# The order of turning and multiplying in the patch stage of a vision tower

## The reference, in short

```python
x = features.reshape(B, c, h, P1, w, P2)
x = jnp.transpose(x, (0, 2, 4, 3, 5, 1)).reshape(B, h * w, P1 * P2 * c)
x = _layernorm(x, ln1_g, ln1_b)
x = jnp.einsum('bnd,de->bne', x, W) + b     # 768 -> 192
x = _layernorm(x, ln2_g, ln2_b)
```

## Time and profile before

| | |
|---|---|
| time, median of 3 runs | 3089.83 us (3086.55 to 3103.68) |
| time of the profiled execution | 3087.19 us |
| its span, first to last instruction | 3085.5 us |
| mean granted TensorE clock | 0.961 |
| busy: TensorE, VectorE, ScalarE, GpSimd | 89%, 75%, 61%, 55% of the span |
| patch stage | to about 368 us |

### The profile page before, as it was taken

One profiled execution on the slowest core, in us unless ns is written; L12 is line 12 of the kernel. 1 busy time (PEld: TensorE's weight loads), 2 busy tenths in 40 slices (PEclk: granted clock), 3 DMA queues, 4 the chain that ended last, 5 costly groups with the idle time before them and its releaser, 6 DMA issues. The chain is left out here.

```text
span 3085.5 us, 95504 instructions
## 1 busy us (share of the span) xinstructions
PE 2732.0 (89%) x31491; PEld 2124.6 (69%) x31491; DVE 2311.9 (75%) x5326; ACT 1878.1 (61%) x3798; POOL 1682.0 (55%) x1957
## 2 busy tenths in 40 slices
PE   5798788999899998989998967999986999999998
PEld 5688645555555555555555546899975888888887
DVE  5689678788878887877788735877765777777776
ACT  5577556667666666666666636777753444444443
POOL 3467635555455666667666432567674444444444
PEclk9899989999999999999999968999987999999999
DMA  6555256676766667676767635444433444444443
GB/s 159 161 157 166 58 121 155 145 164 149 157 142 152 165 163 167 161 173 160 175 159 174 143 76 136 147 147 147 143 126 91 68 67 65 68 67 65 69 66 47
DMA packets 515433, 395.07 MB, mean 128 GB/s; under 512 B 223136, under 2 KB 488386, under 8 KB 515138
## 3 DMA queue, kind: packets, MB, share of 16 engines
q1 hardware_dynamic: 431426, 310.47, 41.3%
q0 software_dynamic: 38496, 46.38, 8.5%
q10 hardware_dynamic: 45216, 34.34, 4.6%
HBM read 232.59 MB, written 155.42 MB: 126 GB/s over the span
## 5 line engine op out<-in xcount | busy, mean ns | idle before, releaser
L814 DVE TENSOR_REDUCE a_mx<-a_mxp 98x4 f32<-98x784 f32 x768 | 747.0, 973 | 268.6 <-PE a_mxp L1000 265.9
L603 ACT ACTIVATE a_pt<-a_st 98x784 f32<-98x784 f32 x768 | 634.6, 826 | 352.8 <-PE a_st L986 351.9
L1817 POOL DMA_INDIRECT out_dram<-f_yo,f_idg x202 | 330.9, 1638 | 415.6 <-DVE f_yo L2158 378.9
L500 POOL TENSOR_TENSOR a_cf<-a_ctxs,a_rec 128x1176 f32<-128x1176 f32 x64 | 171.6, 2681 | 448.1 <-DMA a_rec<-a_recip 448.1
L1895 ACT ACTIVATE f_hf<-f_bank,f_b1c 128x256 f32<-128x256 f32 x606 | 254.3, 473 | 236.0 <-PE f_bank L1128 236.0
L1015 PE MATMUL a_pv<-a_pt,a_vp 98*32 98x196 f32 x6144 | 358.7, 352 | 5.0 <-issue 4.1
L986 PE MATMUL a_st<-a_qst,a_kst 49*128 49x196 f16 x3072 | 266.7, 253 | 78.6 <-DMA a_qst<-a_mrow 53.5
L2320 PE MATMUL f_bank<-f_w2h,f_hh 128*128 x1212 | 298.9, 247 | 19.0 <-DVE f_hl L2142 18.7
L2321 PE MATMUL f_bank<-f_w2h,f_hl 128*128 x1212 | 298.2, 246 | 0.0
L2322 PE MATMUL f_bank<-f_w2l,f_hh 128*128 x1212 | 298.2, 246 | 0.0
L1000 PE MATMUL a_mxp<-a_kst,a_qst 48*128 48x196 f16 x3072 | 263.6, 250 | 28.8 <-DVE a_mx L814 21.5
(11 more groups left out here) (314 smaller groups left out, 8269.9 us busy)
## 6 DMA issues: line engine op xcount, KB each, us to landing
a_rec<-a_recip SPq DMA_DIRECT2D x256, 147.0 KB, 4.9
t_rows<-in_x_dram SPq DMA_DIRECT2D x84, 392.0 KB, 5.7
a_qst<-a_qk SPq DMA_DIRECT2D x256, 110.2 KB, 3.2
a_kst<-a_qk SPq DMA_DIRECT2D x256, 110.2 KB, 4.0
f_xg<-f_listed SPq DMA_DIRECT2D x101, 264.0 KB, 2.8
a_qk<-a_qkh SPq DMA_DIRECT2D x128, 196.0 KB, 3.1
a_qk<-a_qkl SPq DMA_DIRECT2D x128, 98.0 KB, 3.4
a_qk<-a_qkh SPq DMA_DIRECT2D x128, 98.0 KB, 2.5
```

The costliest lines, as they stand in the source:

```text
L603: act.activation(pt[k % PT][:].rearrange("p j a t -> p j (a t)"), st_ps[0:half_t, :, 0:unit_t], ACT.Exp, scale=sm_scale).then_inc(exp_s, 1)
L814: dve.tensor_reduce(mx[:, a, :, 2 * p:2 * p + 2].rearrange("p q j -> p j q"), mx_ps[0:half_t, :, 0:unit_t].rearrange("p j (q t) -> p j q t ...
L1817: pool.indirect_dma_start(out, bass.IndirectOffsetOnAxis(ap=idg[i % 3][:, t:t + 1], axis=0), yo[i % 3][:, t, :], None, compute_op=ALU.add) ...
```

## The change

Within a step TensorE first turned both patches of unit s + 1 and then multiplied both patches of unit s. Now it turns patch 0, multiplies patch 0, turns patch 1, multiplies patch 1. All instructions, waits and signals stay; `yp_s` is still given once, behind the products of patch 1.

```diff
             def step(s, kinds):
-                if "B" in kinds:
-                    u = s + 1
-                    for t in range(2):
+                for t in range(2):
+                    if "B" in kinds:
+                        u = s + 1
                         wait(pe, xn_s, 2 * u + t + 1)
                         wait(pe, xl_s, 2 * (u - 1) + t + 1)
                         for k in range(KT):
                             a, kk = divmod(k, KT // 2)
                             ins = pe.transpose(turned[t][:, a, kk * R:(kk + 1) * R], xn[t][:, k * 128:(k + 1) * 128], ident[0:R, 0:R])
                         ins.then_inc(tr_s, 1)
-                if "C" in kinds:
-                    u, b = s, s % 2
-                    for t in range(2):
+                    if "C" in kinds:
+                        u, b = s, s % 2
                         wait(pe, xl_s, 2 * u + t + 1)
                         if t == 0:
                             wait(pe, yn_s, 2 * (u - 1))
                         ins = products(pe, yp[b][0:R, t * dim:(t + 1) * dim],
                                        [(x[b][t][:, k, :], m[:, k, :]) for k in range(KT) for x, m in ((xh, wh), (xh, wl), (xl, wh))]
                                        + [(first_two[:], brow_parts[:])])
-                    ins.then_inc(yp_s, 1)
+                        if t == 1:
+                            ins.then_inc(yp_s, 1)
```

## The result

| | before | after |
|---|---|---|
| median of 20 runs each | 3090.66 us (3072.61 to 3111.17) | 3109.22 us (3091.80 to 3122.66) |
| ratio after / before | | 1.0047, 95% interval 1.0026 to 1.0067 |
| profiled execution | 3087.19 us | 3092.7 us |
| its span | 3085.5 us | 3091.0 us |
| start of the first `yn` | 46.99 | 46.15 |

The change costs 0.47% by the ratio of the runs (14.5 us of 3090.66; the interval is 8 to 21 us); the two medians lie 18.6 us apart, inside that interval. The patch stage ends 12.8 us later. The single profiled execution hides it in part: its rest, which the change does not touch, happened to be 7.3 us shorter.

The account below looks back on a forecast made before the run. A closed GpSimd-ScalarE loop (4.94 us a clean step) was taken as the bound. Terms 0.4 + 1.5 + 2.0 + 12 + 0.1 = +16.0 us on the profiled 3087.2 gave 3103, range 3090 to 3120.

Parts of the forecast that it names:

- The new loop: ScalarE to TensorE and back, with patch 0's products ahead of T1, sets the step at 5.60 us.
- The signs: Middle stretch: expected waits of `xh`, `yn` and GpSimd, clean steps of 5.5 to 5.7 us, 39 steps about 230 us.
- The work beside: Middle stretch: weight preparation and next-stage first units on all engines, not covered by the longer loop, add 12 us.
- Filling: Start of the patch stage: the moved block delays the first steps, +0.4 us, between 0 and 1.57.
- Three steps before the weights: Steps from 46.99 until SyncE reaches the weights at 62.32: 15.33 us becomes 16.8, +1.5.
- Late rows: Third group's image rows, queued behind weight loads on SyncE, come about 2 us later; later steps before the stall are hidden.
- Restart: After the stall for image rows: a block of slow-clock products stands before T1, +2.0 us.
- Tail: Last steps of the patch stage: two steps lose what the shorter path to the last product returns, +0.1 us.
- The bound before: Before the change, GpSimd and ScalarE's `yn` wait for each other in a closed loop, 4.94 us a clean step.
- second rival: Middle stretch: work beside is not absorbed, 25.7 us on top and 3.9 for the ends, about 3117 us; chance 0.18.
- The clock: TensorE: no slow-clock cost taken for 1.2 us waits; a rival had fallback costing +29 us, 3132, chance 0.06.
- case 1: Likeliest outcome: the ScalarE-TensorE loop sets the step, 3096 to 3112 us, centre 3103; chance 0.60.

Follow-up runs that it names:

- e3: Changed kernel with 10 of patch 0's 19 products between the two turns, the other 9 behind the second turn; 3083.91 us (median of 12), ratio 0.9975.
- e4: Changed kernel with all 19 products of patch 0 and 10 of patch 1 between the two turns; 3148.53 us (one time).
- e8: Changed kernel with `yn` ahead of the second `xh` on ScalarE and the products' statistics ahead of the second `xl` on VectorE; 3102.55 us (one time).
- e7: Changed kernel with GpSimd computing scale and shift ahead of its work on `yn`; 3100.71 us (one time).
- after_again: Changed kernel without any edit, profiled a second time on another, slower chip; its 56th `yn` starts at 377.89 us.
- e2: Kernel before the change with `yn` placed between the first and the second `xh` on ScalarE; 3105.15 us (one time).
- e5: Kernel before the change with GpSimd computing scale and shift ahead of its work on `yn`; 3083.74 us (one time).

## Why the prediction was right

Direction, mechanism and size held: 3103 predicted, 3109.2 measured, +16 against +14.5 us (8 to 21; 18.6 between the medians). Of the 6 us between the times 3.5 are the starting point: the forecast counts from the one profiled execution (3087.2), and the median of 20 runs is 3090.66. That +16 lies so near is in part luck: the patch stage, to which all of its terms belong, ends 12.8 us later in the first pair of profiles and 9.6 in the second. By its steps:

- **The new loop.** Right, with 5.48 us instead of 5.60. The first four terms came out as the rows of before had them, within 0.01 us; T1 to second `xh` was 0.77 for 0.83, and `xh` to `yn` 0.61 for 0.69. For the first of them the reason is in the rows: the prediction counted from the start of T1's weight loading (PEld, 293.75 in the earlier trace rows), and in the loop the first of these loads lies beside the last product: it starts at 289.51, T1's matmuls at 289.60. So 0.09 of the term was in P0 already, and 0.86 from that load to the second `xh` is near the 0.83 of before. That T1 sets it is shown by e3 and e4, that it closes through the order on ScalarE and VectorE by e8, that GpSimd has left it by e7.
- **The signs.** `xh` waits 64.1 us (55 or more expected), `yn` 1.4 for the shift (nearly nothing), GpSimd 60.1 for `yn` (about 70); clean steps 5.48 (5.5 to 5.7); 39 steps 228.1 (about 230).
- **The work beside.** 14.4 us not covered, where the terms gave 12. Two errors offset each other in part: 39 x 0.12 = 4.7 less by the loop, 2.4 more by the work beside; the middle stretch grew by 9.8 and not by 12. Of the 2.4, some 1.6 are the lower clock in the one step of 7.56; without it that step would be about as long as in after_again (5.91). How the 12 split among the engines, no run tests.
- **Filling.** +0.4 expected, the first `yn` came 0.8 earlier. It lies at 45.4 in e2, with the old order, and at 47.2 in e7, with the new one: the spread is larger than the term.
- **Three steps before the weights.** 46.15 to 62.59 is 16.44 for 15.33, +1.1 (+1.5 expected).
- **Late rows.** They were expected about 2 us later and came 0.3 us earlier, since SyncE reached the weights 0.3 later and the rows came 50.6 us after that instead of 51.2. The wrong step is the one to SyncE's queue: the first `yn`, 0.8 earlier, took back most of the 1.1 of the three steps.
- **Restart.** From the late rows to the 12th `yn` 9.30 us, before 6.88: +2.4 (+2.0 expected). The block ahead of T1 runs at the lower level there, as forecast, and takes 3.04 us (P0 at 121.27, T1 at 124.31).
- **Tail.** From the 51st `yn` to the last 25.59 for 24.64: +0.95 (+0.1 expected). Its five steps are 5.48, 5.48, 5.48, 4.58 and 4.57 us, before 5.46, 5.18, 4.59, 4.84 and 4.57: three are in the loop, where I had counted two, and only 0.26 comes back.
- **The bound before.** The weakest part, though the sum did not need it: I took the closed GpSimd loop for what sets the pace. It is the floor of clean steps alone (e5); what sets the average of 5.60 stays open. The second rival, in which the work beside comes on top of the longer loop in full, is out: that would be 39 x 5.48 + 25.7 = 239.4 for the 39 steps, and 228.1 and 228.1 were measured.
- **The clock.** In clean steps no product is 0.16 us from the next, as predicted; the granted clock of the stretch is 0.99. It is not absent, as the 7.56 us step shows; there the lower clock costs about 1.6 us, a term that the forecast had only as "some cold products". The wait in a clean step was forecast as 1.2 us and is 0.97. The Trainium skill ("TensorE: Matmul & The Clock Gate", "HAM oscillation — how this bites in real kernels") says that waits between groups of matmuls can bring the half rate back again and again. The runs agree for waits of 1.79 us (e4, every third step where nothing lies beside) and not for those of 0.97 in the changed kernel.
- **The chances.** Half of case 1 with cases 2 and 3 adds up to 0.54 for slower, not to 0.50, and the rest to 0.41 for same, not to 0.45.
- **What stays open.** The patch stages of the two pairs give +12.8 and +9.6, the timed runs +14.5 with an interval that holds both. Whether the rest of the program adds anything can't be told: from before to after it was 7.3 us shorter in one pair and 17.6 longer in the other.

## What to carry to other kernels

Before moving a block ahead of another on one engine, ask which instruction waits for the later one and what stands behind that instruction in its own engine's order; walk that path from start to start until it closes, and compare its length with the step: the block is free up to the difference. Here the loop without the block is 5.48 - 1.58 = 3.90 us against a step of 4.94, so by an estimate some 12 products are free; 10 were, 19 were not. A floor read from the clean steps tells where a longer loop begins to cost, but not what a shorter one would give; take the loop away in an experiment before counting on it. The largest step forward in the patch stage lay in neither order but in a queue: weights that were wanted late had been put in front of image rows that were wanted at once.

## What the runs showed of the hardware that I had not expected

- A wait of 0.97 us on TensorE in each clean step of 5.48 us left the granted clock up (0.99 over 228 us). With 1.79 us in each step of 6.31 us it fell in every third step, not in each and not in none (0.94 over the 39 steps of e4), and each fall lengthened the step by 1.65 us. Where and whether it falls is not fixed by the wait ahead: in the same step of two profiles of the changed kernel, after 1.83 and 1.84 us, it fell once and once not.
- The hand-over from ScalarE's `xh` to its next `yn` is 0.61 us from start to start here, and 0.69 in the earlier trace rows, for the same two instructions, and neither `yn` has a wait named ahead of it; the copy itself is recorded with 0.72 us.
